# An LSTM recurrence on one core: products that stream 32 repeated columns, and two unread matmuls per step

## The reference

```
x = x + L0(x, cond)    # (x * ys) @ W, each output channel times d; ys = cond / 16, d = rsqrt(ys^2 @ W^2 + eps)
x = x + L1(x)          # LSTM over 1024 steps, hidden size 256, h0 = cond, c0 = 0
L1: xW = x @ Wx + b                     # for all steps
    a = xW[t] + h @ Wh                  # (2, 1024): gates i, f, o, g, 256 each
    i, f, o = sigmoid(a_i, a_f, a_o);  g = tanh(a_g)
    c = f * c + i * g;  h = o * tanh(c) # h is the output of step t
```

## Time and profile before

| | |
|---|---|
| median of 3 executions | 2079.24 us |
| the profiled execution: its own time, its span | 2078.44 us, 2076.7 us |
| mean granted TensorE clock over the span | 0.522 |
| busy: TensorE matmuls, weight loads | 91%, 84% |
| busy: VectorE, ScalarE, GpSimd | 61%, 34%, 24% |
| identity matmuls, products | 12288, 45056 |

### The profile page before, as it was taken

How to read it: one execution, slowest core, us unless ns; L and a number is a source line. 1 busy time by engine, 2 the same in 40 slices (tenths; PEclk the granted TensorE clock), 3 DMA queues, 4 the chain that set the end, 5 groups by cost and what they waited for, 6 DMA issues and landing times.

```text
span 2076.7 us, 141184 instructions
## 1 busy us (share of the span) xinstructions
PE 1879.6 (91%) x57580; PEld 1740.1 (84%) x57580; DVE 1268.8 (61%) x8384; ACT 697.9 (34%) x5149; POOL 499.1 (24%) x1291
## 2 busy tenths in 40 slices
PE   8999999999999999999999999999999999999997
PEld 5588888888888888888888888888888888888887
DVE  3366666666666666666666666666666666666665
ACT  2233333333333333333333333333333333333333
POOL 1122222222222222222222222222222222222221
PEclk9855555555555555555555555555555555555555
DMA  2000000000000000000000000000000000000000
GB/s 86 2 1 1 1 1 1 1 1 1 1 1 1 1 1 1 1 1 1 1 1 1 1 1 1 1 1 1 1 1 1 1 1 1 1 1 1 1 1 1
DMA packets 20368, 6.67 MB, mean 3 GB/s; under 512 B 17532, under 2 KB 19848, under 8 KB 20360
## 3 DMA queue, kind: packets, MB, share of 16 engines
q1 hardware_dynamic: 20088, 6.30, 1.3%
q10 hardware_dynamic: 272, 0.26, 0.0%
HBM read 4.46 MB, written 2.10 MB: 3 GB/s over the span
## 4 chain that ended last, share of the span: by engine, by line
PE 71%; DVE 14%; ACT 9%; issue 5%; DMA 0%; SPq 0%; POOLq 0%; POOL 0%; DVEq 0%
PE psum L292 71%; DVE psum L583 10%; ACT scan_in L660 9%; DVE psum L576 4%; DMA wh_sb<-in_L_cond_Wh_dram 0%; PE psum L315 0%; ACT xw L639 0%; DVE wh_sb L467 0%; SPq L182 0%; SPq L183 0%; POOLq L56 0%; PE psum L342 0%; POOL y_cols L243 0%; DVE y_rows L597 0%; DVE y_rows L602 0%
## 5 line engine op out<-in xcount | busy, mean ns | idle before, releaser
L292 PE MATMUL psum<-h_parts,wh_p 128*128 128x2 f16 (+1 forms) x45056 | 1371.1, 166 | 0.0
L292 PEld LDWEIGHTS psum<-h_parts,wh_p 128*128 128x128 f16 x45056 | 1287.2, 104 | 16.5
L292 PE MATMUL psum<-ring,ident_b 128*128 128x4 bf16 (+2 forms) x12288 | 492.3, 168 | 185.0 <-DVE psum L583 183.3
L292 PEld LDWEIGHTS psum<-ring,ident_b 128*128 128x128 bf16 x12288 | 408.5, 105 | 269.7 <-DVE psum L583 267.2
L657 ACT ACTIVATE sig_f<-psum 128x4 f32<-128x4 f32 x1024 | 178.2, 174 | 1127.6 <-DVE psum L574 1127.6
L574 DVE TENSOR_REDUCE psum<-psum 128x4 f32<-128x8 f32 x1024 | 179.2, 175 | 389.8 <-PE psum L292 389.8
L231 POOL CAST ring<-xw 128x64 bf16 (+1 forms) x256 | 121.1, 473 | 1158.7 <-POOLq L269 1124.7
L586 DVE SCALAR_TENSOR_TENSOR h_parts<-scan_h 128x4 f16<-128x4 f32 x1024 | 175.3, 171 | 249.2 <-ACT scan_h L666 249.2
L662 ACT ACTIVATE scan_h<-psum 128x2 f32<-128x2 f32 x1024 | 177.2, 173 | 134.6
L589 DVE TENSOR_TENSOR_SCAN h_parts<-scan_h,h_parts 128x12 f16<-128x12 f32 x1024 | 188.3, 184 | 35.0
L576 DVE TENSOR_REDUCE psum<-psum 128x4 f32<-128x8 f32 x1024 | 179.2, 175 | 39.5
(11 more groups left out here) (75 smaller groups left out, 216.6 us busy)
## 6 DMA issues: line engine op xcount, KB each, us to landing
out_dram<-y_rows SPq DMA_DIRECT2D x512, 4.0 KB
x_rows<-in_x_dram SPq DMA_DIRECT2D x4, 512.0 KB, 8.4
wh_sb<-in_L_cond_Wh_dram SPq DMA_DIRECT2D x1, 1024.0 KB, 5.9
wx_sb<-in_L_cond_Wx_dram SPq DMA_DIRECT2D x1, 1024.0 KB, 11.2
w_sb<-in_L_cond_weight_dram ACTq DMA_DIRECT2D x1, 256.0 KB, 2.7
small_rows<-in_cond_dram SPq DMA_DIRECT2D x1, 2.0 KB
small_rows<-in_L_cond_b_dram SPq DMA_DIRECT2D x1, 4.0 KB
```

The costliest lines, as they stand in the source:

```text
L292: return nc.tensor.matmul(out_, lhs, rhs, start=first, stop=last, skip_group_check=True)
```

## The change

WIDE = 32 columns are given to each chunk of each gate, and the banks are laid out anew: I_BANK, G_BANK, F_BANK, O_BANK, O_REST, CELL, and two banks that have become free, KEEP and KEEP_TOO. The small sums move into the gates' own banks, behind column WIDE x K = 64; gate I's chunks lie behind column 64 too, so that one ScalarE instruction can read I and G at equal offsets in two neighbouring banks.

Each product except the last of its call reads its 2 or 4 moving columns over and over (a broadcast with step 0), 16 or 8 times, and writes all 32 columns of its chunk. The repeated columns hold copies that nobody reads. The last product of a call writes the 2 or 4 columns alone. There are 7 calls in a step, so 37 products of 44 become wide.

Two matmuls are added to a step, both with the identity as weights and as moving data. One of 2 x 32 = 64 columns goes to KEEP_TOO, behind the last identity matmul and ahead of the wait for h_hi. One of 2 x 128 = 256 columns goes to KEEP, behind the last product. No instruction reads these banks.

```diff
@@ -31,13 +31,14 @@
 HALF = UNROLL // 2
 EPS = 1e-8
 QUAD = 32
+WIDE = 32
 H_SCALE = 12
 W_TOP = 14
 EXPONENT = 0x7F800000
 GATE_I, GATE_F, GATE_O, GATE_G = range(4)
 
-I_BANK, G_SUM, F_BANK, O_BANK, G_BANK, FO_SUM, CELL, O_REST = range(8)
+I_BANK, G_BANK, F_BANK, O_BANK, O_REST, CELL, KEEP, KEEP_TOO = range(8)
 BANK_OF_GATE = (I_BANK, F_BANK, O_BANK, G_BANK)
 
@@ -102,7 +103,7 @@
         scan_in = sb("scan_in", [P, 6 * CB + 2 + 2])
         scan_a = scan_in[:, 0:3 * CB].rearrange("p (c s) -> p c s", s=3)
         scan_b = scan_in[:, 3 * CB + 2:6 * CB + 2].rearrange("p (c s) -> p c s", s=3)
-        sig_ig = scan_in[:, 2:6 * CB + 2].rearrange("p (h c s) -> p h c s", h=2, s=3)[:, :, :, 0]
+        sig_ig = scan_in[:, 2:6 * CB + 2].rearrange("p (h c b s) -> p h c b s", h=2, b=B, s=3)[:, :, :, :, 0]
 
         scan_h = sb("scan_h", [P, CB, 3])
@@ -113,10 +114,16 @@
         psum = ctx.enter_context(nc.psum_tensor("psum", [P, 8, BANK], F32))
         banks = [psum[:, i, :] for i in range(8)]
-        pre_f = banks[FO_SUM][:, 0:CB]
-        pre_o = banks[FO_SUM][:, CB:CB + B]
-        pre_g = banks[G_SUM][:, 0:CB]
-        pre_ig = psum[:, I_BANK:G_SUM + 1, 0:CB]
+        def wide(bank, first, last):
+            return banks[bank][:, WIDE * first:WIDE * last].rearrange("p (c n) -> p c n", n=WIDE)
+
+        def behind(bank):
+            return banks[bank][:, WIDE * K:2 * WIDE * K].rearrange("p (c n) -> p c n", n=WIDE)[:, :, 0:B]
+
+        pre_f = banks[F_BANK][:, WIDE * K:WIDE * K + CB]
+        pre_o = banks[O_BANK][:, WIDE * K:WIDE * K + B]
+        pre_g = behind(G_BANK)
+        pre_ig = psum[:, I_BANK:G_BANK + 1, WIDE * K:2 * WIDE * K].rearrange("p h (c n) -> p h c n", n=WIDE)[:, :, :, 0:B]
         cell = banks[CELL][:, 0:3 * CB].rearrange("p (c s) -> p c s", s=3)
 
@@ -373,11 +380,13 @@
             def apart(gate, first, last):
-                return banks[BANK_OF_GATE[gate]][:, 2 * B * first:2 * B * last].rearrange("p (c q b) -> p c q b", q=2, b=B)
+                return wide(BANK_OF_GATE[gate], first, last)[:, :, 0:2 * B].rearrange("p c (q b) -> p c q b", q=2)
             def together(bank, first, last):
-                return banks[bank][:, B * first:B * last].rearrange("p (c b) -> p c b", b=B)
+                if bank == I_BANK:
+                    first, last = first + K, last + K
+                return wide(bank, first, last)[:, :, 0:B]
             def in_ring(gate, u, part, first, last):
                 return ring[:, u, gate, part, B * first:B * last].rearrange("p (c b) -> p c b", b=B)
@@ -394,14 +403,28 @@
                     mm_ = mm(together(bank, first, last), ident_b[:, :], in_ring(gate, u, part, first, last), part == 0, True)
                 return mm_
+            def spread(bank, c, moving):
+
+                if bank == I_BANK:
+                    c += K
+                columns = wide(bank, c, c + 1)[:, 0, :]
+                if len(moving.shape) > 2:
+                    copies = WIDE // (2 * B)
+                    return columns.rearrange("p (r q b) -> p r q b", r=copies, b=B), moving.unsqueeze(1).broadcast_to([P, copies, 2, B])
+                copies = WIDE // B
+                return columns.rearrange("p (r b) -> p r b", b=B), moving.unsqueeze(1).broadcast_to([P, copies, B])
+
             def products(gate, bank, h_part, first, last):
                 for c in range(first, last):
                     m = gate * K + c
                     for k in range(K):
+                        moving = h_parts[:, h_part, k * B:(k + 1) * B, 2]
+                        columns, copies = spread(bank, c, moving)
                         for w_part in range(2):
-                            mm_ = mm(together(bank, c, c + 1)[:, 0, :], wh_p[:, w_part, k, m * P:(m + 1) * P],
-                                     h_parts[:, h_part, k * B:(k + 1) * B, 2], False, True)
+                            if (c, k, w_part) == (last - 1, K - 1, 1):
+                                columns, copies = together(bank, c, c + 1)[:, 0, :], moving
+                            mm_ = mm(columns, wh_p[:, w_part, k, m * P:(m + 1) * P], copies, False, True)
                 return mm_
             def products_apart(gate, first, last):
@@ -409,10 +432,18 @@
                 for c in range(first, last):
                     m = gate * K + c
                     for k in range(K):
+                        moving = h_parts[:, :, k * B:(k + 1) * B, 2]
+                        columns, copies = spread(BANK_OF_GATE[gate], c, moving)
                         for w_part in range(2):
-                            mm_ = mm(apart(gate, c, c + 1)[:, 0, :, :], wh_p[:, w_part, k, m * P:(m + 1) * P],
-                                     h_parts[:, :, k * B:(k + 1) * B, 2], False, True)
+                            if (c, k, w_part) == (last - 1, K - 1, 1):
+                                columns, copies = apart(gate, c, c + 1)[:, 0, :, :], moving
+                            mm_ = mm(columns, wh_p[:, w_part, k, m * P:(m + 1) * P], copies, False, True)
                 return mm_
+
+            def keep_streaming(bank, copies, columns):
+
+                mm(banks[bank][:, 0:copies * columns].rearrange("p (r n) -> p r n", n=columns), ident_b[:, :],
+                   ident_b[:, 0:columns].unsqueeze(1).broadcast_to([P, copies, columns]), True, True)
             for gate_mm in (f_mm, g_mm, o0_mm, o_mm):
                 pe.sem_inc(gate_mm, 1)
@@ -431,6 +462,7 @@
                     last = input_together(GATE_O, O_REST, u, 1, K)
                     if u % HALF == HALF - 1:
                         last.then_inc(ring_used, 1)
+                    keep_streaming(KEEP_TOO, 2, WIDE)
                     pe.wait_ge(h_hi, t + u + 1)
                     products(GATE_I, I_BANK, 0, 0, K)
                     pe.wait_ge(h_lo, t + u + 1)
@@ -440,6 +472,7 @@
                     products_apart(GATE_O, 0, 1).then_inc(o0_mm, 1)
                     products(GATE_O, O_REST, 0, 1, K)
                     products(GATE_O, O_REST, 1, 1, K).then_inc(o_mm, 1)
+                    keep_streaming(KEEP, 2, P)
         @block.vector
         def _(dve):
@@ -552,7 +585,7 @@
             def parts_of(gate, chunks):
-                return banks[BANK_OF_GATE[gate]][:, 0:2 * B * chunks].rearrange("p (c q b) -> p c b q", b=B, q=2)
+                return wide(BANK_OF_GATE[gate], 0, chunks)[:, :, 0:2 * B].rearrange("p c (q b) -> p c b q", q=2)
             def by_chunk(ap):
                 return ap.rearrange("p (c b) -> p c b", b=B)
@@ -573,7 +606,7 @@
                     dve.wait_ge(f_mm, step)
                     nc.vector.tensor_reduce(by_chunk(pre_f), parts_of(GATE_F, K), AX.X, ALU.add).then_inc(f_sum, 1)
                     dve.wait_ge(g_mm, step)
-                    nc.vector.tensor_reduce(by_chunk(pre_g), parts_of(GATE_G, K), AX.X, ALU.add).then_inc(ig_in, 1)
+                    nc.vector.tensor_reduce(pre_g, parts_of(GATE_G, K), AX.X, ALU.add).then_inc(ig_in, 1)
                     dve.wait_ge(f_act, step)
                     nc.vector.tensor_tensor(scan_b[:, :, 2], sig_f[:, :], cell[:, :, 2], ALU.mult).then_inc(cell_in, 1)
                     dve.wait_ge(o0_mm, step)
@@ -661,7 +694,7 @@
                     act.wait_ge(o0_sum, step)
                     nc.scalar.activation(scan_h[:, 0:B, 1], pre_o, ACT.Sigmoid, scale=unscale).then_inc(o0_act, 1)
                     act.wait_ge(o_mm, step)
-                    nc.scalar.activation(scan_h[:, B:CB, 1], banks[O_REST][:, B:CB], ACT.Sigmoid, scale=unscale).then_inc(o_act, 1)
+                    nc.scalar.activation(scan_h[:, B:CB, 1], wide(O_REST, 1, K)[:, 0, 0:B], ACT.Sigmoid, scale=unscale).then_inc(o_act, 1)
                     act.wait_ge(c_done, step)
                     nc.scalar.activation(scan_h[:, :, 2], cell[:, :, 2], ACT.Tanh).then_inc(t_done, 1)
 
```

## The result

The changed kernel took 2101.22 us (median of 4 runs, 2100.35 to 2101.60), the kernel before 2079.47 on the same chip; the ratio is 1.0104, with a 95% interval of 1.0093 to 1.0116. Forecast were 2037 us and a range of 2028 to 2086: the sign and the time were wrong.

A forecast was written before the change was run, and what follows sets the result against it. The prediction took a per-step ring through 24 TensorE products at half clock, plus VectorE, ScalarE and handovers, as the bound; 1021 periods x 41 ns = 41.9 us less than 2078.44 gave 2036.5, median 2037 us, range 2028 to 2086.

The forecast's parts named there:

- I take: it rises and is held: TensorE's clock in the recurrence: 1572 streamed columns a step raise it from half to full and keep it there.
- What the full clock is worth: Path of one step at full instead of half clock: 38 to 46 ns saved, 41 ns taken, 2.1% of a step.
- The working by the path: L589's end to L660's start: 0.90 us now, 0.85 to 0.86 at full clock from handover, pause, 23 spacings and lag.
- The other working: Products on the path: 23 spacings shrink from 27.3 to 25.3 ns, at most 46 ns a step.
- Wider products: I take 0: 37 products streaming 32 columns hide behind the next weight load: cost 0, upper bound 53 ns at half clock.
- The unread matmuls: 64 columns before the wait for h, 256 behind the last product: both covered, cost 0; at most 53 ns and 0.21 us.
- The PSUM places: Reductions and L660 reading the new bank layout: cost 0, bounds 0 to 7 ns for L660.
- Rival B: Clock stays at 1.2 GHz and all is hidden: 2079 us, to 2083 with the layout; chance 0.17.
- Rival C: Load and stream of 16-bit products don't overlap whole, clock stays low: 2099 us at one cycle a product; chance 0.18.
- Rival A: Clock swings, some steps at full and some at half; half and half gives 2058 us; chance 0.15.
- The rule against this: Trainium skill's 81 ns per load and 128-column matmul: 32-column pairs near 41 ns, step slower by some 0.3 us.

The follow-up runs named there:

- e5: Changed kernel with the two parts of h 32 bytes apart instead of 24: 2076.79 us, ratio 0.9992.
- e10: Changed kernel with 512 instead of 256 unread columns behind the last product, h_parts left in its old place: 2078.07 us, ratio 0.9996.
- e8: Changed kernel with parts of h 32 bytes apart and 512 instead of 256 unread columns behind the last product: 2040.70 us (one run).
- e9: Changed kernel with parts of h 32 bytes apart, 40-column chunks, 80 unread columns before the wait, 512 and 128 behind the last product: 2034.65 us, ratio 0.9786.
- e4: Changed kernel with only the products of the low part alone (8 in gate I, 4 in O's second chunk) narrow again: 2078.92 us, ratio 0.9999.
- e12: Changed kernel with h_parts laid out so the first chunk's columns of both high and low part cross a multiple of 32 bytes: 2465 us (one run).
- e1: Changed kernel without its two unread matmuls: 2106.52 us, ratio 1.0131.
- e2: Changed kernel with all products narrow, new PSUM places and both unread matmuls kept: 2079.58 us, ratio 1.0001.
- e7: Changed kernel with parts of h 32 bytes apart and four unread matmuls of 512 columns behind the last product instead of one of 256: 2450.75 us (one run).
- e3: Changed kernel with h_parts moved by 32 bytes in SBUF: 2107.68 us, ratio 1.0137.
- e11: Changed kernel with all products narrow, parts of h 32 bytes apart, 768 instead of 256 unread columns behind the last product: 2336.69 us (one run).
- e6: Changed kernel with parts of h 32 bytes apart, 56-column chunks, 112 and 512 unread columns instead of 64 and 256: 2084.05 us, ratio 1.0026.

## Why the prediction was wrong, step by step

**"I take: it rises and is held": wrong, and this is the step that failed.** The clock of the changed kernel fell in the second step and stayed at 0.50 to the end. Even without the slow products it is up for 4% of the time (e5, mean 0.52). The same kernel with 512 unread columns instead of 256, and nothing else changed, has it up for 74% (e10), and with the parts of h 32 bytes apart besides for 94% (e8) or, with 40-column chunks and 640 unread columns, throughout (e9). So what the change streams did not suffice, and the trace before could not show by how much it fell short: the step was argued from two ends with nothing between them, and it carried the whole forecast. The lower of these ends, the 7 us of weight loads with 2-column streams, rested on their spacing of 214 ns alone. The clock rows of the kernel before read 1.00 there too, which the prediction doesn't mention:

```profile
10.00:12.00 2.00, 2.00 (x11) 2.00 (x11) 1.35 (x6) 0.20 (x1) 0.00 (x0) 1.00 1.13 361
```

**What the full clock is worth: right by the path, wrong by the spacing.** 41 ns a step and 1.892 us were forecast; e9 measured 41.6 and 1891.7 ns, and its 2034.65 us is near the 2037 given for a clock that holds. The working by the path holds term by term, within 10 ns each (means from the traces): from the end of h's second part to product 9 73 ns before and 57 in e9, from there to product 32 620 and 591, from there to the sigmoid 202 and 210, together 0.895 and 0.858 us. The other working, 23 spacings of 27.3 ns that become 25.3, does not: the even spacing is 26.7 at half clock and 25.0 at full, and the stretch from product 9 to product 32 gave 29 ns, not 38 to 46. The rest came from the start of product 9, 16 ns sooner, less 8 ns for the sigmoid, and 4 to 5 ns in the tanh and the handovers beside it. That the 41 came out to within 1 ns is partly luck, as it was picked between 38 and 46.

**"Wider products: I take 0": wrong for one call, the seven wide products of gate I with the low part, of 21 wide products on the path.** This is the step that made the kernel slower instead of equal. The fp32 rows showed that a stream as long as its load is hidden when its columns lie in a row. The change streams two columns over and over, and for the first chunk of the low part these lie on two sides of a multiple of 32 bytes. That costs 21.5 ns in seven spacings, 28.3 to 33.3 ns instead of 26.7. e5 puts the 0 back, e4 shows the same from the other side, e12 brings the slowness to other calls by the place alone.

**The unread matmuls: right.** The thin cover of the 64 columns held (e1, e2; L619's end to the first product unchanged). **The PSUM places: right**, L693 took its 181 ns.

**Rival B** had the clock right (0.50) and gave 2079, which is what e4 measures, the kernel without the one slow call. **Rival C** had the time (2099) and the sign, but by luck: its mechanism, a handover between load and stream in each product, is not what happened, as 14 of the wide products on the path start as evenly as before. The forecast's range, up to 2086, left C's 2099 out although C had a chance of 0.18. **Rival A**, the swinging clock, occurs in e5, e8 and e10, but not in the changed kernel. A and C are linked, which I had not seen: what makes the step slower also takes the clock away (e10 against e8). **The rule against this** did not show: in e9 16-bit pairs with 40 columns start every 25.0 to 25.2 ns at full clock, and 32 columns every 25.0 to 25.3 (e7). The Trainium skill ("TensorE: Matmul & The Clock Gate", section "Back-to-back issue gap") has 81 ns for a pair with 128 columns, from which some 41 for 32 was estimated; these runs don't bear the estimate out, and no run has 16-bit products of 128 columns. The Trainium skill, "TensorE: Matmul & The Clock Gate", section "A second HAM failure mode: psum-queue depth-cycling", describes such swings of another kernel, put down to short idle gaps; e8's rows show the swings, and no run here shows that gaps cause them.

Open: whether the piece that a repeated pair must not leave is 16 or 32 bytes long; why the same tanh takes 176 ns in one kernel and 180 in another (6 ns a step in e1 and e3); and why the price of a crossing is 2 to 7 ns with two pieces and 12 to 36 with four.

## What to carry to other kernels

Price a clock change in two parts, what it would be worth and whether it comes, and give the second a chance of its own when the trace shows only the extremes; here the first was right and the second wrong. A padded or repeated stream isn't free because it is short: look at which bytes it repeats. Every pair here that cost nothing lay within one aligned piece of 16 bytes; whether 32 is enough wasn't tested. When a filler is meant to hold the clock, size it for the idle stretch at full clock, since that is where it has to fit (512 columns in 0.21 us, against an idle stretch of 0.34), and check the granted clock over the whole run: e11 shows what a filler of 768 columns costs where the clock stays down, 257 us.

## What the runs showed of the hardware

- Repeating two 16-bit columns on two sides of a multiple of 32 bytes, 32 columns in all: 28 to 33 ns between products instead of 26.7 at half clock (after, e3), and 28 to 32 instead of 25.0 at full clock (e10). Four columns in four pieces: 39 to 62 ns (e12). Four columns of which two lie together in a piece: 26.7 (after, e5).
- The spacing of 16-bit pairs at full clock: 25.0 to 25.3 ns with 32 or 40 columns (e7, e8, e9) and 25.3 by the timeline with 2 and 4 (first step before), mostly 27.5 with 56 (e6), though 56 columns last only 23.3 ns.
- A clock that swings many times in one run (e5, e8, e10), with its mean, 0.52, 0.97 and 0.87. Between e8 and e10 it moved by 0.10 through spacings that are a few ns longer in two calls.
